# A top-2 mixture of experts: from all experts on all tokens to expert-sorted tiles with accumulating DMAs

## The chip, the cores and the metric

The kernel runs on one core of a Trainium2 chip. The metric is the device time of an execution in microseconds, the median of several runs.

## The reference

Eight sublayers in a row work on x of 4 x 256 tokens by 256 features, each as x = x + f(layernorm(x)): linear attention, mixture of experts, a convolution with a scan, the same mixture of experts again, softmax attention, attention with a routed feed-forward, delta-rule attention, and attention with a routed feed-forward again. The change is to the mixture of experts (8 experts, top 2 of them, hidden size 512), which is run twice with the same weights:

```python
x = hidden_states.reshape(-1, H)                      # 1024 tokens, H = 256
logits = SOFTCAP * jnp.tanh(x @ w_gate / SOFTCAP)     # 8 experts
probs = jax.nn.softmax(logits, axis=-1)
_, idx = jax.lax.top_k(probs, TOPK)                   # TOPK = 2
weights = probs * jax.nn.one_hot(idx, E).sum(-2)
for e in range(E):
    h = jax.nn.silu(x @ w1[e]) * (x @ w3[e])
    out = out + h @ w2[e] * weights[:, e:e + 1]
```

## The kernel before

x lives in SBUF for the whole kernel as X (128 partitions, 8 blocks of tokens, 256). `norm` writes the normalized tokens to XN and, transposed with TensorE, to XT. Each sublayer is a Stage with its own buffers and semaphores; it ends with `all_engine_barrier` (L87), so no work of one stage starts before the last of the one before it. DMAs in flight are held up by it only if an engine waits for them.

`moe` starts with the router: 16 small matmuls (L425), tanh and exp on ScalarE, then a chain of small VectorE operations (`Chain.then`: each waits for the one before it), with `top2` among them, that leaves `weight` (the probability, or zero) for every token and expert.

Then all 8 experts run over all 1024 tokens. SyncE loads an expert's w1, w3 and w2 (1.5 MB) into one of two halves of W, two experts ahead of need. Every FP32 operand is split in two fp32r parts: ScalarE casts (L476, L483, L488) and GpSimd subtracts to get the rest (L513, L518, L524). Each product is three passes (PASSES). For an expert there are 8 groups (2 halves of the tokens, 4 blocks of the hidden size) of 12 matmuls at L444, 512 columns each, then SiLU on ScalarE (L495) and the product on VectorE (L558); then 8 blocks of tokens with 12 matmuls of 256 columns at L457, each block added to X with its weight by VectorE (L562). Experts 0 and 1 are written out, the other six run in a loop.

`linear_attention` is the stage before the first mixture: L250 and L257 are its matmuls with plain FP32 operands, the first with 12 jobs of 2 matmuls. `setup` loads X and makes `ident`; its SyncE waits for X. `conv_scan` follows the first mixture. `routed_ffn` has a router of its own that calls `top2`; L956 are transposes of the softmax attention, L1635 is a small GpSimd operation in the delta attention, L562 has a register in its address.

## Time and profile before

| | |
|---|---|
| Median of 3 runs | 3173.69 us (3169.89 to 3178.28) |
| The profiled execution, its own time | 3158.17 us |
| Its span, first to last instruction | 3156.5 us |
| Mean granted clock of TensorE | 0.842 |
| TensorE matmul busy | 2496.7 us (79%) |
| TensorE weight load busy | 2058.7 us (65%) |
| VectorE, ScalarE, GpSimd busy | 1757.7, 1215.6, 1385.2 us |
| DMA | 198.73 MB, mean 63 GB/s |

PE is TensorE's matmuls and PEld its weight loads, DVE VectorE, ACT ScalarE, POOL GpSimd, SP SyncE; a q behind a name is that engine's queue or sequencer. Times are microseconds from the span's start unless they are marked otherwise. A granted clock of 1.00 is 2.4 GHz, 0.50 is 1.2 GHz. A busy share over the whole span averages stages that run one after the other and are limited by different things, so each stage has to be read by itself.

### The profile page before, as it was taken

How to read it: one execution, taken by the hardware profiler on the slowest of the kernel's cores; microseconds unless marked ns; L12 is line 12 of the kernel's file. 1: busy time of each engine (PE TensorE's matmuls, PEld its weight loads, DVE VectorE, ACT ScalarE, POOL GpSimd, SP SyncE). 2: the span in 40 equal slices, each digit the busy share in tenths (PEclk: the TensorE clock that was granted, in tenths of full speed). 3: DMA queues.
4: the chain of work that ended last, by engine and by line, in shares of the span. 5: the costliest groups of instructions: out<-in, count | busy, mean ns of one | idle time of the engine just before them, and what ended most of it. 6: DMA issues, size and time to landing. Idle time of an engine off the chain costs nothing. (4 is left out here: it accounts for less than half of the span.)

```text
span 3156.5 us, 45390 instructions
## 1 busy us (share of the span) xinstructions
PE 2496.7 (79%) x16778; PEld 2058.7 (65%) x16778; DVE 1757.7 (56%) x3323; ACT 1215.6 (39%) x2736; POOL 1385.2 (44%) x1063
## 2 busy tenths in 40 slices
PE   6699846999797988957478966796679857759798
PEld 4689725888474667846466855686567746627687
DVE  2422375222455553366867776776687687445533
ACT  2333232333241333336344643464345534213233
POOL 0454313454201005536964496637692696310064
PEclk9799967999898998979587967697668957779899
DMA  0210002110000005033321232223223332010050
GB/s 30 81 61 20 0 17 80 41 40 0 17 1 19 1 5 194 0 74 110 121 88 68 78 124 95 86 92 97 97 81 105 95 128 81 31 45 1 36 164 14
DMA packets 121569, 198.73 MB, mean 63 GB/s; under 512 B 60049, under 2 KB 94753, under 8 KB 116257
## 3 DMA queue, kind: packets, MB, share of 16 engines
q1 hardware_dynamic: 121376, 196.21, 19.2%
q8 instruction: 115, 1.88, 0.2%
q14 instruction: 78, 0.63, 0.1%
HBM read 192.38 MB, written 3.81 MB: 62 GB/s over the span
## 5 line engine op out<-in xcount | busy, mean ns | idle before, releaser
L444 PE MATMUL PS<-XP_moe,WP_moe 128*128 128x512 f32 x1536 | 355.3, 392 | 30.8 <-POOL WP_moe L518 28.6
L444 PEld LDWEIGHTS PS<-XP_moe,WP_moe 128*128 128x128 f32 x1536 | 289.6, 189 | 91.6 <-issue 28.7
L1792 PE MATMUL PS<-ident,XT 128*128 128x128 f32 x512 | 115.1, 408 | 244.8 <-DVE XT L2164 230.4
L2106 DVE SCALAR_TENSOR_TENSOR XT<-M_delta,CW_delta,XT 128x256 f32<-128x256 f32 x576 | 249.9, 495 | 71.3 <-ACT M_delta L1975 41.2
L1792 PEld LDWEIGHTS PS<-ident,XT 128*128 128x128 f32 x512 | 92.3, 211 | 264.3 <-DVE XT L2164 126.3
L1741 PE MATMUL PS<-XP_delta,X 128*128 128x268 f32 (+1 forms) x1024 | 242.0, 390 | 6.6 <-DMA X<-in_L_attn_b_heads 6.5
L558 DVE TENSOR_TENSOR HF_moe<-SG_moe,PS 128x512 f32<-128x512 f32 x128 | 87.9, 688 | 265.3 <-ACT SG_moe L495 265.2
L1741 PEld LDWEIGHTS PS<-XP_delta,X 128*128 128x128 f32 x1024 | 193.6, 190 | 56.5 <-issue 11.3
L524 POOL TENSOR_TENSOR HP_moe<-HF_moe,HP_moe 128x512 fp32r<-128x512 f32 x128 | 163.6, 1292 | 138.2 <-ACT HP_moe L488 138.2
L1019 ACT ACTIVATE PR_attn<-PS,NM_attn 128x256 f32<-128x256 f32 (+1 forms) x384 | 135.2, 419 | 224.0 <-DVE NM_attn L1079 224.0
L1256 PE MATMUL PS<-XP_rffn,UW_rffn 128*128 128x512 f32 x816 | 194.9, 396 | 4.7 <-POOL UW_rffn L1212 4.6
L1212 POOL TENSOR_TENSOR UW_rffn<-W_rffn,UW_rffn 128x512 fp32r<-128x512 f32 x34 | 43.8, 1287 | 327.0 <-ACT UW_rffn L1315 327.0
L457 PEld LDWEIGHTS PS<-WP_moe,HP_moe 128*128 128x128 f32 x1536 | 186.4, 192 | 1.2
L1680 POOL TENSOR_TENSOR DD_delta<-DD_delta,A_delta 128x64 f32<-128x64 f32 (+6 forms) x224 | 170.0, 759 | 39.2 <-ACT A_delta L2063 19.5
L457 PE MATMUL PS<-WP_moe,HP_moe 128*128 128x256 f32 x1536 | 186.8, 283 | 0.0
L1256 PEld LDWEIGHTS PS<-XP_rffn,UW_rffn 128*128 128x128 f32 x816 | 155.9, 192 | 38.5 <-issue 5.9
L945 PE MATMUL PS<-KM_attn,QK_attn 128*128 128x512 f32 x288 | 163.5, 650 | 18.7 <-DVE KM_attn L1055 18.7
L1064 DVE COPY PT_attn<-PS 128x512 f32<-128x512 f32 x144 | 99.6, 692 | 130.6 <-PE PS L956 130.6
L495 ACT ACTIVATE SG_moe<-PS 128x512 f32<-128x512 f32 x128 | 76.6, 599 | 233.8 <-PE PS L444 233.1
L1706 POOL TENSOR_TENSOR M_delta<-M_delta,DD_delta 128x2304 f32<-128x2304 f32 x32 | 164.9, 5154 | 0.0
L518 POOL TENSOR_TENSOR WP_moe<-W_moe,WP_moe 128x3072 fp32r<-128x3072 f32 x16 | 108.8, 6808 | 127.6 <-ACT WP_moe L483 127.6
L1805 PEld LDWEIGHTS PS<-XN,KQ_delta 16*128 16x128 f32 (+2 forms) x3072 | 154.5, 306 | 7.3 <-issue 7.3
(314 smaller groups left out, 5636.5 us busy)
## 6 DMA issues: line engine op xcount, KB each, us to landing
M_delta<-gram_delta SPq DMA_DIRECT2D x32, 2304.0 KB, 8.8
X<-in_L_attn_b_heads SPq DMA_DIRECT2D x64, 512.0 KB, 3.3
W_moe<-in_L_ffn_w SPq DMA_DIRECT2D x48, 512.0 KB, 4.8
CB_rffn<-routes_rffn SPq DMA_DIRECT2D x20, 512.0 KB, 23.6
XN<-in_L_attn_b_outs SPq DMA_DIRECT2D x16, 512.0 KB, 3.7
F_delta<-in_L_attn_b_outs SPq DMA_DIRECT2D x4, 2048.0 KB, 8.2
W_rffn<-in_L_ffn_tiles SPq DMA_DIRECT2D x4, 1536.0 KB, 11.6
W_rffn<-in_L_ffn_tiles SPq DMA_DIRECT2D x2, 2304.0 KB, 27.0
```

Of the source, the lines that this page charges most:

```text
L444: last = nc.tensor.matmul(PS[:, 2 * (g % 2) + i, :], up_w(qw, r, i, k, m), XP[qx][:, k, n * NB:(n + 1) * NB], start=(k + step == 0), stop= ...
L457: last = nc.tensor.matmul(PS[:, 4 + i % 4, 0:D], HP[qx][:, k, i * P:(i + 1) * P], down_w(qw, r, k), start=(k + step == 0), stop=(k == MI - ...
L524: nc.gpsimd.tensor_tensor(HP[1][:, m, n * NB:(n + 1) * NB], HF[:, g % 4, :], HP[0][:, m, n * NB:(n + 1) * NB], ALU.subtract).then_inc(hl_d, 1)
L945: nc.tensor.matmul(bank, QK[:, 0, kt, b * T + qt * P:b * T + (qt + 1) * P], KM[:, kt, h:h + per, b * T:b * T + keys], start=True, stop=False)
L1019: last = nc.scalar.activation(PR[:, u % 4, j * w:(j + 1) * w], PS[:, u % 3, j * w:(j + 1) * w], ACT.Exp, bias=NM[:, u % 4, j:j + 1])
L1256: last = nc.tensor.matmul(PS[:, 4 + 2 * n + q, :], UW[qw][:, r, (q * KD + k) * P:(q * KD + k + 1) * P], XP[qx][:, k, n * NB:(n + 1) * NB], ...
L1680: last = nc.gpsimd.tensor_tensor(DD[:, :, tri(t - 1) + 1:tri(t)], DD[:, :, tri(t):tri(t + 1)], step(t).broadcast_to([P, BH, C - t]), ALU.mult)
L1706: nc.gpsimd.tensor_tensor(q, q, by_h(DD[:]), ALU.mult).then_inc(mq_d, 1)
L1741: last = nc.tensor.matmul(PS[:, 1 + i, 0:B * (WIN - halo)], WH[:, r, i, k, :], XP[:, k, :, n * BT + halo:n * BT + WIN], start=(k == 0), st ...
L1792: last = nc.tensor.transpose(PS[:, 6 + r % 2, i * P:(i + 1) * P], W[:, B * h:B * (h + 1), :], core.ident[:])
L1805: last = nc.tensor.matmul(PS[:, 1 + b, h * 2 * C:(h + 1) * 2 * C].rearrange("p (q t) -> p q t", q=2), WT(o)[rows, h, :], GR[rows, o, h].re ...
L2106: nc.vector.scalar_tensor_tensor(TMP[:, r, i], RAW[:, r, i, :, tau:tau + BT], CW[:, i, h, tau:tau + 1], TMP[:, r, i], ALU.mult, ALU.add).t ...
```

## The change

The mixture computes only the chosen pairs of token and expert. The 2048 pairs are sorted by expert into slots in DRAM, each expert's share padded up to a multiple of 128, which needs at most 23 tiles of 128 slots (SLOTS = 2944).

- The weights of all 8 experts (12.6 MB) are loaded into SBUF once (`EW`), by 24 DMAs that SyncE issues in `linear_attention` behind that stage's own, and both mixtures use them. EW stays allocated until the second mixture is done.
- `setup` fills the slots in DRAM with a padding row (zeros, a row number past the tokens, 1032 bytes), writes a padding block behind `sums`, and now also waits for this second write, which is queued behind the fill.
- `moe`: SyncE also writes X to `sums` in DRAM. The router and `top2` are as before. TensorE counts the chosen pairs with nine bf16 products, VectorE works out each pair's slot and each tile's expert (`owner`). GpSimd issues 16 indirect DMAs, one for each block of tokens and rank, that scatter the normalized tokens with row number and weight (XW) to the slots. When all have landed SyncE loads the 23 tiles back in 5 groups (XS).
- TensorE reads the 23 owners into registers, and for each tile transposes the tokens (2), makes gate and up products (2 matmuls of 512 columns each, plain FP32), transposes the hidden rows (4), and makes the down product (4 matmuls of 256 columns). The weights' address depends on the register. ScalarE does SiLU and scales the answer, VectorE the product and the copies out of PSUM.
- GpSimd adds each tile's answers to the tokens' rows of `sums` with one indirect accumulating DMA, and waits for each to land before it issues the next. When all 23 have landed SyncE loads X back from `sums`. In the first mixture SyncE fills the slots again, behind the loads of the tiles.
- In `conv_scan` CUM no longer has a buffer of its own but lies in XP. `top2` returns the one-hot pair, and the two operations that followed it are in its callers.

The diff, with the removed lines of `moe` (all in the printed function above) and the allocations left out:

```diff
...
+EXPERT = 512
+SLOTS = 2 * N + (E - 1) * P
...
+    def expert_weights(self, ctx):
+        nc = self.nc
+        self.EW = ctx.enter_context(nc.sbuf_tensor("EW", [P, E, 3 * KD * EXPERT], FP32))
+        self.pad = ctx.enter_context(nc.sbuf_tensor("pad", [P, D + 2], FP32))
+        self.row_id = ctx.enter_context(nc.sbuf_tensor("row_id", [P, NT + 1], FP32))
+        self.slots = nc.dram_tensor("slots", (SLOTS, D + 2), FP32, kind="Internal").ap()
+        self.sums = nc.dram_tensor("sums", (N + P, D), FP32, kind="Internal").ap()
...
+    def fill_slots(self, sp):
+        sp.dma_start(self.slots.rearrange("(t p) d -> p t d", p=P),
+                     self.pad[:].unsqueeze(1).broadcast_to([P, SLOTS // P, D + 2])).then_inc(self.zeroed, 16)
+    def load_experts(self, sp):
+        if self.asked:
+            return
+        self.asked = True
+        I = EXPERT
+        for e in range(E):
+            for i, (w, k, n) in enumerate((("w1", KD, I), ("w3", KD, I), ("w2", I // P, D))):
+                sp.dma_start(self.EW[:, e, i * KD * I:(i + 1) * KD * I].rearrange("p (k n) -> p k n", k=k),
+                             self.a["L0_ffn_" + w][e].rearrange("(k p) n -> p k n", p=P)).then_inc(self.expert_in, 16)
...
         def _(sp):
             sp.dma_start(core.X[:], core.a["L0_attn_a_x"].rearrange("b (i p) d -> p (b i) d", p=P)).then_inc(x_in, 16)
-            sp.wait_ge(x_in, 16)
...
+            core.fill_slots(sp)
+            sp.dma_start(core.sums[N:N + P], core.pad[:, 0:D]).then_inc(x_in, 16)
+            sp.wait_ge(x_in, 32)
...
         def _(pool):
+            nc.gpsimd.memset(core.pad[:], 0.0).then_inc(filled, 1)
+            nc.gpsimd.iota(core.row_id[:], [[P, NT + 1]], base=0, channel_multiplier=1,
+                           allow_small_or_imprecise_dtypes=True).then_inc(filled, 1)
...
+            nc.gpsimd.tensor_copy(core.pad[:, D:D + 1], core.row_id[:, NT:NT + 1]).then_inc(filled, 1)
...
         def _(sp):
...
                 sp.dma_start(W[:, i], a["L0_attn_a_" + name].rearrange("(k p) n -> p k n", p=P)).then_inc(w_in, 16)
+            core.load_experts(sp)
...
-def top2(core, s, dve, c, p, weights, rank):
+def top2(core, s, dve, c, p, rank):
...
             src = rest
-    c.then(nc.vector.tensor_tensor(oh[:, 0], oh[:, 0], oh[:, 1], ALU.add))
-    return nc.vector.tensor_tensor(weights, oh[:, 0], p[:], ALU.mult)
+    return oh
 def moe(core, a="L0_ffn_"):
...
+    I = EXPERT
...
+    TILES = SLOTS // P
...
+    GROUPS = (0, 1, 3, 7, 13, TILES)
...
         def _(sp):
...
+            sp.dma_start(sums, X[:]).then_inc(base_out, 16)
+            core.load_experts(sp)
+            sp.wait_ge(g_in, 16)
+            sp.wait_ge(placed, 32 * NT * (layer_no + 1))
+            for i in range(len(GROUPS) - 1):
+                at = slice(GROUPS[i], GROUPS[i + 1])
+                sp.dma_start(XS[:, at], slots[:, at]).then_inc(x_in[i], 16)
+            for i in range(len(GROUPS) - 1):
+                sp.wait_ge(x_in[i], 16)
+            if layer_no == 0:
+                core.fill_slots(sp)
+            sp.wait_ge(added, 16 * TILES * (layer_no + 1))
+            sp.dma_start(X[:], sums).then_inc(x_back, 16)
+            sp.wait_ge(x_back, 16)
+        @block.gpsimd
+        def _(pool):
+            c = Chain(pool, chain_p)
+            nc.gpsimd.memset(ones[:], 1.0)
+            nc.gpsimd.memset(lower[:], float(P))
+            c.then(nc.gpsimd.memset(before[:], 1.0))
+            nc.gpsimd.affine_select(out=before[:], in_=before[:], compare_op=ALU.is_ge, fill=0.0, base=-1,
+                                    pattern=[[1, P]], channel_multiplier=-1).then_inc(consts, 1)
+            nc.gpsimd.affine_select(out=lower[:], in_=lower[:], compare_op=ALU.is_ge, fill=0.0, base=-1,
+                                    pattern=[[1, E], [-1, E]], channel_multiplier=0).then_inc(consts, 1)
+            pool.wait_ge(slot_d, 1)
+            pool.wait_ge(core.zeroed, 16 * (layer_no + 1))
+            pool.wait_ge(rows_d, 2)
+            for i in range(NT):
...
+                    nc.gpsimd.indirect_dma_start(
+                        core.slots[:], bass.IndirectOffsetOnAxis(ap=slot[:, r, i:i + 1], axis=0),
+                        XW[:, r, i], None).then_inc(placed, 16)
+            pool.wait_ge(base_out, 16)
+            for t in range(TILES):
+                if t in GROUPS:
+                    pool.wait_ge(token_d, GROUPS.index(t) + 1)
+                pool.wait_ge(y_ev, t + 1)
+                if t or layer_no:
+                    pool.wait_ge(added, 16 * (TILES * layer_no + t))
+                nc.gpsimd.indirect_dma_start(core.sums[:], bass.IndirectOffsetOnAxis(ap=token[:, t:t + 1], axis=0),
+                                             XS[:, t, 0:D], None, compute_op=ALU.add).then_inc(added, 16)
...
         def _(pe):
...
+            pe.wait_ge(consts, 2)
+            pe.wait_ge(pick_d, 1)
+            m = picked[:].rearrange("p i e -> p (i e)")
+            nc.tensor.matmul(PS[:, 6, 0:NT * E], ones[:], m, start=True, stop=True).then_inc(sum_mm, 1)
+            nc.tensor.matmul(PS[:, 5, 0:NT * E], before[:], m, start=True, stop=False)
+            for i in range(1, NT):
+                last = nc.tensor.matmul(PS[:, 5, i * E:NT * E], ones[:], m[:, 0:(NT - i) * E], start=False, stop=i == NT - 1)
+            last.then_inc(sum_mm, 1)
+            pe.wait_ge(owner_d, 1)
+            e = [pe.value_load(owner[0:1, t:t + 1], min_val=0, max_val=E - 1) for t in range(TILES)]
+            pe.wait_ge(core.expert_in, 48 * E)
+            def turn(t):
+                if t in GROUPS:
+                    pe.wait_ge(x_in[GROUPS.index(t)], 16)
+                if t:
+                    pe.wait_ge(xk_d, t)
+                for k in range(KD):
+                    last = nc.tensor.transpose(PS[:, 0, k * P:(k + 1) * P], XS[:, t, k * P:(k + 1) * P], core.ident[:])
+                last.then_inc(xt_mm, 1)
+            def gate(t):
+                pe.wait_ge(xk_d, t + 1)
+                if t >= 2:
+                    pe.wait_ge(silu_d, t - 1)
+                for k in range(KD):
+                    last = nc.tensor.matmul(PS[:, 2 + 2 * (t % 2), :], XK[:, t % 3, k],
+                                            EW[:, bass.ds(e[t], 1), k * I:(k + 1) * I].rearrange("p o n -> p (o n)"),
+                                            start=(k == 0), stop=(k == KD - 1))
+                last.then_inc(gate_mm, 1)
+            def up(t):
+                if t >= 2:
+                    pe.wait_ge(h_d, t - 1)
+                for k in range(KD):
+                    last = nc.tensor.matmul(PS[:, 3 + 2 * (t % 2), :], XK[:, t % 3, k],
+                                            EW[:, bass.ds(e[t], 1), (KD + k) * I:(KD + k + 1) * I].rearrange("p o n -> p (o n)"),
+                                            start=(k == 0), stop=(k == KD - 1))
+                last.then_inc(up_mm, 1)
+            def turn_hidden(t):
+                pe.wait_ge(h_d, t + 1)
+                if t:
+                    pe.wait_ge(ht_d, t)
+                for k in range(MI):
+                    last = nc.tensor.transpose(PS[:, 1, k * P:(k + 1) * P], H[:, t % 2, k * P:(k + 1) * P], core.ident[:])
+                last.then_inc(ht_mm, 1)
+            def down(t):
+                pe.wait_ge(ht_d, t + 1)
+                if t >= 2:
+                    pe.wait_ge(y_ev, t - 1)
+                for k in range(MI):
+                    at = 2 * KD * I + k * D
+                    last = nc.tensor.matmul(PS[:, 6 + t % 2, 0:D], HT[:, t % 2, k],
+                                            EW[:, bass.ds(e[t], 1), at:at + D].rearrange("p o n -> p (o n)"),
+                                            start=(k == 0), stop=(k == MI - 1))
+                last.then_inc(dn_mm, 1)
+            turn(0)
+            turn(1)
+            for t in range(TILES):
+                gate(t)
+                if t:
+                    turn_hidden(t - 1)
+                up(t)
+                if t + 2 < TILES:
+                    turn(t + 2)
+                if t:
+                    down(t - 1)
+            turn_hidden(TILES - 1)
+            down(TILES - 1)
...
         def _(act):
+            nc.scalar.copy(XW[:, 0, :, 0:D], XN[:])
+            nc.scalar.copy(XW[:, 1, :, 0:D], XN[:]).then_inc(rows_d, 1)
...
+            def answer(t):
+                act.wait_ge(dn_mm, t + 1)
+                nc.scalar.activation(XS[:, t, 0:D], PS[:, 6 + t % 2, 0:D], ACT.Copy,
+                                     scale=XS[:, t, D + 1:D + 2]).then_inc(y_ev, 1)
+            for t in range(TILES):
+                act.wait_ge(gate_mm, t + 1)
+                if t >= 2:
+                    act.wait_ge(h_d, t - 1)
+                nc.scalar.activation(SG[:, t % 2], PS[:, 2 + 2 * (t % 2), :], ACT.Silu).then_inc(silu_d, 1)
+                if t:
+                    answer(t - 1)
+            answer(TILES - 1)
...
         def _(dve):
...
+                nc.vector.memset(rank[:, e:e + 1], float(E - e))
+                last = nc.vector.memset(edges[:, e:e + 1], float(P * e))
+            for t in range(TILES):
+                last = nc.vector.memset(tile_at[:, t:t + 1], float(P * t))
...
+            oh = top2(core, s, dve, c, prob, rank)
+            nc.vector.tensor_tensor(picked[:], oh[:, 0], oh[:, 1], ALU.add).then_inc(pick_d, 1)
+            c.then(nc.vector.tensor_tensor(chosen[:], oh[:], prob[:].unsqueeze(1).broadcast_to([P, 2, NT, E]), ALU.mult))
+            c.then(nc.vector.tensor_reduce(weight[:], chosen[:], AX.X, ALU.add))
+            nc.vector.tensor_copy(XW[:, :, :, D + 1], weight[:])
+            for r in range(2):
+                last = nc.vector.tensor_copy(XW[:, r, :, D], core.row_id[:, 0:NT])
+            last.then_inc(rows_d, 1)
+            dve.wait_ge(sum_mm, 1)
+            dve.wait_ge(consts, 2)
+            c.then(nc.vector.tensor_reduce(count[:], PS[:, 6, 0:NT * E].rearrange("p (i e) -> p e i", e=E), AX.X, ALU.add))
+            c.then(nc.vector.tensor_tensor(over[:], count[:].unsqueeze(2).broadcast_to([P, E, E]),
+                                           edges[:].unsqueeze(1).broadcast_to([P, E, E]), ALU.is_gt))
+            c.then(nc.vector.tensor_reduce(used[:], over[:], AX.X, ALU.add))
+            c.then(nc.vector.tensor_tensor(over[:], lower[:], used[:].unsqueeze(1).broadcast_to([P, E, E]), ALU.mult))
+            c.then(nc.vector.tensor_reduce(base[:], over[:], AX.X, ALU.add))
+            dve.wait_ge(sum_mm, 2)
+            c.then(nc.vector.tensor_tensor(place[:], PS[:, 5, 0:NT * E].rearrange("p (i e) -> p i e", e=E),
+                                           base[:].unsqueeze(1).broadcast_to([P, NT, E]), ALU.add))
+            c.then(nc.vector.tensor_tensor(chosen[:], oh[:], place[:].unsqueeze(1).broadcast_to([P, 2, NT, E]), ALU.mult))
+            c.then(nc.vector.tensor_reduce(where[:], chosen[:], AX.X, ALU.add))
+            nc.vector.tensor_copy(slot[:], where[:]).then_inc(slot_d, 1)
+            c.then(nc.vector.tensor_tensor(past[:], tile_at[:].unsqueeze(2).broadcast_to([P, TILES, E - 1]),
+                                           base[:, 1:E].unsqueeze(1).broadcast_to([P, TILES, E - 1]), ALU.is_ge))
+            c.then(nc.vector.tensor_reduce(sought[:], past[:], AX.X, ALU.add))
+            nc.vector.tensor_copy(owner[:], sought[:]).then_inc(owner_d, 1)
+            def tokens(i):
+                dve.wait_ge(x_in[i], 16)
+                nc.vector.tensor_copy(token[:, GROUPS[i]:GROUPS[i + 1]], XS[:, GROUPS[i]:GROUPS[i + 1], D]).then_inc(token_d, 1)
+            def columns(t):
+                dve.wait_ge(xt_mm, t + 1)
+                if t >= 3:
+                    dve.wait_ge(up_mm, t - 2)
+                nc.vector.tensor_copy(XK[:, t % 3].rearrange("p k n -> p (k n)"), PS[:, 0, 0:D]).then_inc(xk_d, 1)
+            def hidden_columns(t):
+                dve.wait_ge(ht_mm, t + 1)
+                if t >= 2:
+                    dve.wait_ge(dn_mm, t - 1)
+                nc.vector.tensor_copy(HT[:, t % 2].rearrange("p k n -> p (k n)"), PS[:, 1, :]).then_inc(ht_d, 1)
+            columns(0)
+            columns(1)
+            tokens(0)
+            tokens(1)
+            for t in range(TILES):
+                if t:
+                    hidden_columns(t - 1)
+                dve.wait_ge(up_mm, t + 1)
+                dve.wait_ge(silu_d, t + 1)
+                if t >= 2:
+                    dve.wait_ge(ht_mm, t - 1)
+                nc.vector.tensor_tensor(H[:, t % 2], SG[:, t % 2], PS[:, 3 + 2 * (t % 2), :], ALU.mult).then_inc(h_d, 1)
+                if t + 2 < TILES:
+                    columns(t + 2)
+                if t + 2 in GROUPS[2:-1]:
+                    tokens(GROUPS.index(t + 2))
+            hidden_columns(TILES - 1)
...
-    CUM = s.sb("CUM", [P, KD, N])
+    CUM = XP[:].rearrange("p k b t -> p (k b t)")[:, 0:KD * N]
...
-            c.then(nc.vector.tensor_tensor_scan(flat(CUM), KEEP[:], flat(VR), 0.0, ALU.mult, ALU.add))
+            c.then(nc.vector.tensor_tensor_scan(CUM, KEEP[:], flat(VR), 0.0, ALU.mult, ALU.add))
...
-            c.then(nc.vector.tensor_tensor(flat(VR), flat(CUM), flat(A2), ALU.mult))
+            c.then(nc.vector.tensor_tensor(flat(VR), CUM, flat(A2), ALU.mult))
...
-            top2(core, s, dve, c, prob, weight[:, :, 0:E], rank).then_inc(route_d, 1)
+            oh = top2(core, s, dve, c, prob, rank)
+            c.then(nc.vector.tensor_tensor(oh[:, 0], oh[:, 0], oh[:, 1], ALU.add))
+            nc.vector.tensor_tensor(weight[:, :, 0:E], oh[:, 0], prob[:], ALU.mult).then_inc(route_d, 1)
...
 def program(nc, args, out):
...
         core = Core(nc, ctx, args)
...
+        core.expert_weights(experts)
...
         subs = [sub1, sub2, sub3, sub2, sub5, sub6, sub7, sub6]
-        for f in subs[START:STOP]:
+        for i, f in enumerate(subs[START:STOP]):
             f()
+            if START + i == min(3, STOP - 1):
+                experts.close()
...
```

## Rows read from the trace of the kernel before

**Rows 1.** Busy time by stretch (windows), all engines; the header names the columns.

```profile
core 0: us, PE busy (x) PEld busy (x) DVE busy (x) ACT busy (x) POOL busy (x), PEclk, DMA share, GB/s
...
121.90:383.80 261.90, 261.23 (x1512) 231.86 (x1512) 74.23 (x127) 87.26 (x132) 122.51 (x70) 1.00 0.09 30
89.90:99.00 9.10, 6.88 (x32) 6.88 (x32) 0.00 (x0) 0.95 (x1) 0.00 (x0) 0.50 0.87 274
...
820.00:1060.00 240.00, 205.63 (x1045) 0.91 0.02 7
```

**Rows 2.** Timeline where the first mixture stage ends and the second begins and ends.

```profile
384.48 1.28 ACT L196 ACT_TABLE_LOAD   x1 [10.82 <-PEq L87]
...
501.06 0.37 SPq L403 DMA_DIRECT2D WG_moe<-in_L_ffn_w_gate  x1
...
794.79 1.28 ACT L196 ACT_TABLE_LOAD   x1 [10.83 <-PEq L87]
```

**Rows 3.** Timeline of the first mixture stage's start: start, us, engine, line, op, tiles.

```profile
89.56 0.37 SPq L403 DMA_DIRECT2D WG_moe<-in_L_ffn_w_gate  x1
...
99.49 0.22 DVE L544 TENSOR_REDUCE mx_moe<-logit_moe 128x8 f32<-128x64 f32 x1 [9.59 <-ACT logit_moe L471]
...
100.16 1.88 ACT L476 CAST XP_moe<-XT 128x2048 fp32r<-128x2048 f32 x1
...
102.32 4.42 DVE L358 SCALAR_TENSOR_TENSOR top_rest_moe<-top_oh_moe,prob_moe 128x64 f32<-128x64 f32 x1
...
113.42 7.54 PE L444 MATMUL PS<-XP_moe,WP_moe 128*128 128x512 f32 x24 [14.30 <-POOL WP_moe L518]
118.28 0.60 ACT L495 ACTIVATE SG_moe<-PS 128x512 f32<-128x512 f32 x1 [9.63 <-PE PS L444]
...
125.61 0.69 DVE L558 TENSOR_TENSOR HF_moe<-SG_moe,PS 128x512 f32<-128x512 f32 x1 [3.14 <-ACT SG_moe L495]
```

**Rows 4.** PE's timeline through the experts; one pair of eight.

```profile
149.89 21.95 PE L444 MATMUL PS<-XP_moe,WP_moe 128*128 128x512 f32 x96
171.68 11.68 PE L457 MATMUL PS<-WP_moe,HP_moe 128*128 128x256 f32 x96
183.19 21.95 PE L444 MATMUL PS<-XP_moe,WP_moe 128*128 128x512 f32 x96
```

**Rows 5.** Timeline row and windows of single lines (L250, L257), linear attention.

```profile
28.57 22.57 PE L250 MATMUL PS<-XT,W_linattn 128*128 128x512 f32 x48 [7.76 <-DMA W_linattn<-in_L_attn_a_Wp]
...
36.00:51.00 15.00, 15.00 (x36) 6.43 (x34) 1.00 0.00 0
...
51.00:58.20 7.20, 7.05 (x32) 5.87 (x31) 1.00 0.01 3
```

**Rows 6.** Timeline in the softmax attention, transposes at L956.

```profile
856.75 0.47 PEld L956 LDWEIGHTS PS<-ident,PR_attn 128*128 128x128 f32 x4 [0.33 <-issue]
...
857.19 0.97 PEld L969 LDWEIGHTS PS<-V_attn,PT_attn 128*128 128x128 f32 x8
...
857.50 0.69 DVE L1064 COPY PT_attn<-PS 128x512 f32<-128x512 f32 x1 [1.01 <-PE PS L956]
```

**Rows 7.** Instructions of single lines (L1635, L562): min/median/max ns.

```profile
L1635 POOL TENSOR_TENSOR RT_delta<-RT_delta,LN_delta x32: 1006/1026/1041, 1697.9 to 2752.8; 128x4 f32<-128x4 f32 x32
...
L562 DVEq FUSED_REGOPS  x96: 46/46/46, 206.6 to 793.5; - x96
```

**Rows 8.** DMA issues: count, KB each, median us from issue to landing.

```profile
y_delta<-M_delta SPq DMA_DIRECT2D x4, 256.0 KB, 3.0
X<-spill_delta SPq DMA_DIRECT2D x1, 1024.0 KB, 5.5
...
CB_rffn<-routes_rffn SPq DMA_DIRECT2D x4, 128.0 KB, 11.9
...
WG_moe<-in_L_ffn_w_gate SPq DMA_DIRECT2D x2, 8.0 KB, 2.1
```

**Rows 9.** Timeline, first work behind the setup stage.

```profile
7.01 1.28 ACT L196 ACT_TABLE_LOAD   x1 [7.01 <-PEq L87]
```

More of the change, by code:

```diff
@@ L375, in moe @@
     prob = s.sb("prob", [P, NT, E])
-    weight = s.sb("weight", [P, E, NT])
     rank = s.sb("rank", [P, E])
@@ new lines, in moe @@
+    before = s.sb("before", [P, P], BF16)
+    ones = s.sb("ones", [P, P], BF16)
+    edges = s.sb("edges", [P, E])
+    lower = s.sb("lower", [P, E, E])
+    tile_at = s.sb("tile_at", [P, TILES])
+    count = s.sb("count", [P, E])
+    over = s.sb("over", [P, E, E])
+    used = s.sb("used", [P, E])
+    base = s.sb("base", [P, E])
+    place = s.sb("place", [P, NT, E])
+    chosen = s.sb("chosen", [P, 2, NT, E])
+    slot = s.sb("slot", [P, 2, NT], mybir.dt.uint32)
+    where = s.sb("where", [P, 2, NT])
@@ new lines, in moe @@
+    base_out, x_back, rows_d, token_d = (s.sem(n) for n in ("base_out", "x_back", "rows_d", "token_d"))
+    placed, added, layer_no = core.placed, core.added, core.layer_no
+    core.layer_no += 1
+    x_in = [s.sem(f"x_in{i}") for i in range(len(GROUPS) - 1)]
+    xt_mm, xk_d, gate_mm, up_mm, silu_d, h_d, ht_mm, ht_d, dn_mm, y_ev = (s.sem(n) for n in (
+        "xt_mm", "xk_d", "gate_mm", "up_mm", "silu_d", "h_d", "ht_mm", "ht_d", "dn_mm", "y_ev"))
+    slots = core.slots.rearrange("(t p) d -> p t d", p=P)
@@ L490, in expert @@
-            def expert(j, r, first):
-                for g in range(G):
-                    act.wait_ge(up_mm, (2 * j + r) * G + g + 1)
-                    if not (first and g < 4):
-                        act.wait_ge(h_d, (2 * j + r) * G + g - 3)
-                    nc.scalar.activation(SG[:, g % 4, :], PS[:, 2 * (g % 2), :], ACT.Silu).then_inc(silu_d, 1)
-                    if g:
-                        hidden(j, r, g - 1)
-                hidden(j, r, G - 1)
-            split(0, 0, True)
@@ L2288, in program @@
         core = Core(nc, ctx, args)
+        experts = ExitStack()
+        core.expert_weights(experts)
         setup(core)
```

153 lines of the change are left out of this document (27 added, 126 removed).

## Prediction, made before the change was built or run

> **What bounds the kernel now.** The windows by stage come first [rows 1]. The eight sublayers run one after the other with a barrier behind each, so a stage's gain is whole and nothing outside it moves. The two mixture stages are the stretches from 89.56 us (the router weights' load) to 384.48 us (first work of the next norm) and from 501.06 to 794.79 us [rows 2, 3]: 294.9 and 293.7 us, mean 294.3, together 588.6 of the 3156.5 us span. Within them read PE: from 121.9 us on it is busy 261.2 of 261.9 us at a granted clock of 1.00 [rows 1], each expert costing 21.95 us for 96 matmuls at L444 and 11.68 us for 96 at L457, a period of 33.3 us [rows 4]. Eight experts are 266 us; the other 28 us are routing, splitting the first weights, and a slow start. So PE sets the end, and what counts is how many columns PE streams, plus whatever stands before its first tile and behind its last.
>
> **What is removed.** All 8 x 33.3 us of dense matmuls, with the splits and casts on ACT, DVE and POOL. Those lay beside PE except before the first expert: there PE waits 14.3 us for POOL's split. DVE's routing chain also has an operation stretched to 4.42 us beside POOL's large subtractions, against 0.22 us for another of its size [rows 3]. With no large POOL work in the new stage I expect none of that.
>
> **The tile loop.** The new matmuls take plain FP32 operands in one pass instead of three split ones. The plain FP32 stage shows the price: L250 needs 12 x 2 matmuls of 512 columns and the trace has 48 records, so two records each; a stretch of 15.0 us with PE never idle holds 34 loads and touches 36 matmul records, so some 35 pitches of 0.429 us. L257's 32 records of 256 columns span 7.05 us, 0.220 each [rows 5]. Four transposes in a row start their loads at 856.75 and give way at 857.19: 0.11 us each [rows 6]. A tile has 4 matmuls of 512 columns (8 records, 3.43 us), 4 of 256 (8 records, 1.76) and 6 transposes (0.66): 5.85 us, times 23 is 134.5. I add 3 us per layer for the start (24 matmuls took 7.54 us at first, against 0.227 each later [rows 3, 4]) and 0.15 us a tile for gaps, 3.4: 140.9 us. The order gate(t), turn_hidden(t-1), up(t), turn(t+2), down(t-1) leaves each result of another engine one matmul group of at least 1.7 us: the product on DVE costs 0.69 us, SiLU on ACT 0.60 [rows 3], the copy of the turned hidden rows 0.69 [rows 6]. DVE has at most three such copies and products a tile, 2.1 us, ACT at most 1.2, so neither is late. Register arithmetic for the dynamic weight offset has 46 ns an operation on DVE's sequencer [rows 7]; three or four beside a matmul of 0.44 or 0.86 us stay hidden, and cost some 0.2 us each if they aren't.
>
> **Before the first tile.** From stage start to the first DVE reduction is 9.9 us as before [rows 3]. Its ten small chained operations up to 102.32 with ACT's exponential among them take 2.83 us, so some 0.255 each and 0.3 more; 31 of them come to 8.3 us, and the slots stand 18.2 us after the start. The constants, ACT's two copies of XN (near 1.9 us each by the cast of that size) and PE's nine counting products lie under the router's matmuls and the DVE chain. Then POOL issues 16 indirect scatters one after the other, which no row shows. Below, SP's issue of a DMA is 0.37 us; above, a full landing of 3.0 us each [rows 3, 8]. I take 1.2, just over the 1.03 us that a POOL operation on 4 elements costs [rows 7], its fixed cost: 19.2 us (ends 6 and 48). The last scatter lands 3.0 us later, SP issues the gathers in 0.4, the first two groups land 3.0 later: 6.4. Two transposes and a copy: 1.2. PE's 23 register loads wait only on the owners and lie under the scatters. Sum 45.0 us.
>
> **Behind the last tile.** Product, copy, answer and their hand-overs 1.7; the last accumulating DMA L; SP's issue 0.35, the 1 MB reload of X 5.5 [rows 8], barrier 0.3. For L the bounds are 2.1 us (the landing of an 8 KB load) and 11.9 (a 128 KB broadcast load), the nearest row is the 3.0 us of a 256 KB store; since an addition must read before it writes I take nearly twice that, 5.5 us. Together 13.4.
>
> The Trainium skill ("DMA: Bandwidth & Descriptors", section on the anatomy of a DMA on the SWDGE path) gives such a DMA about 2.0 us plus its bytes over 436 GB/s, an estimate of 2.3 us here; no row of this trace has such a DMA. By it the layer would end 3.2 us sooner and the kernel 6.4 us sooner.
>
> **Outside the stages.** Setup now waits for a 128-row store queued behind a 3.04 MB fill of the slots. At the 274 GB/s of the busiest stretch [rows 1] the fill is 11 us, behind most of X's own load, with which setup ended at 7.0 before [rows 9]; it should now end near 17.5: +10.5 us (ends +5 and +20). The 12.6 MB of expert weights need 46 us at that rate, from 28.6 us on, where the stage's own weights have landed [rows 5], plus the 10.5: done near 85, before the mixture stage's loads, then near 100, want the rings. The second fill and 24 loads less in each layer lie under PE. CUM's new place and the split-up top2 cost nothing: same operations in the same chain.
>
> **Sum.** A layer: 45.0 + 140.9 + 13.4 = 199.3 us against 294.3, so 95.0 less; twice is 190.0; less 10.5 leaves 179.5. The profiled execution took 3158.17 us (span 3156.5), so 2978.7. The median of the three timed runs is 3173.69, 15.5 above it, and carried over that gives **2994 us**.
>
> **Rivals.**
> Rival A, the chain of accumulating DMAs sets the end. Each waits for the one before it, so 23 L run in series. The first answer comes at 45.0 + 3 + two tiles (12.0) + 0.5 = 60.5 us, the last at 187.6, so above L = 5.8 us the chain is the bound, and the layer takes 66.7 + 23 L. My 5.5 is barely under. For it: a row's read, addition and write in series, with 128 KB loads at 11.9 us in this trace; against it: plain stores at 3.0 [rows 8]. At 8 us: 250.7 a layer, 3097 us in all. Chance 0.27 up to the next case.
> Rival B, the same chain on the other side: slower from L = 9.7 us, where 66.7 + 23 L reaches 289. At the 11.9 us bound: 340.4 a layer, 3276 us. Chance 0.05.
> Rival C, dispatch costs more: 3.0 us for each scatter adds 28.8 a layer, 3052 us. Chance 0.05.
> Rival D, PE keeps its lower clock (1.2 GHz) through the loop. A fifth of the tile's instructions are transposes and the groups are short. Against: the attention stretch, mixed in the same way with transposes and waits, was granted 0.91 [rows 1, 6]. The price is PE's 134.5 us again, less the 3 already counted: +131.5 a layer, 3257 us. Chance 0.03.
> The Trainium skill ("TensorE: Matmul & The Clock Gate", Part 4 on transposes) says that transposes don't count as busy PE for the clock in the same way. By that rule D's time would follow if they weighed enough; the trace doesn't bear it out for attention, which stayed at 0.91.
>
> **How the numbers follow.** My own case has 0.60; its range is 2950 (scatters at 0.4 us, no gaps, L of 3, setup +5) to 3035 (scatters at 2.0, setup +20). The whole range goes from 2945 into rival A up to just over L = 8: 3100, leaving out some 0.05 below and 0.13 above. About 0.3% is what a measurement of this kernel can tell. Faster: own case, A and C, 0.92. Slower: B, D and small change, 0.07. Within 0.3%: 0.01.
>
> **What would show it.** In the profile after: L444 and L457 gone; 184 matmuls (368 records) and 138 transposes a layer in some 138 us at clock near 1.00; PE idle from the counting products for about 29 us while POOL's queue shows 16 issues; accumulating DMAs spaced at PE's pace (6 us), not at their own landing time. If they are evenly spaced above 6 us, and PE's last tile ends well before the last of them, A was right and the step "L" was mis-sized. If the tile period is near 9 or 12 us with a granted clock of 1.00 or 0.50, the loop's price was. Setup's end tells the fill.

## The result, and the profile after

The changed kernel takes 2977.45 us (median of 4 runs, 2967.05 to 2982.18), the kernel before, run beside it, 3171.79 (4 runs, 3167.83 to 3178.28). The ratio is 0.938, with an interval of 0.935 to 0.941. The forecast was 2994 us in a range of 2945 to 3100: it was 17 us, 0.6%, too high, on the right side and by the right mechanism. The profiled execution took 2972.99 us.

The page of the changed kernel: the head, the costliest group that is new, and the DMA issues. The columns are those of the page before.

```profile
span 2971.3 us, 40960 instructions
...
PE 2231.3 (75%) x14736; PEld 1748.9 (59%) x14736; DVE 1663.0 (56%) x3309; ACT 1082.8 (36%) x2558; POOL 1211.4 (41%) x1008
...
L506 POOL DMA_INDIRECT sums<-XS_moe,token_moe x46 | 71.7, 1560 | 220.6 <-ACT XS_moe L602 201.6
...
EW<-in_L_ffn_w SPq DMA_DIRECT2D x24, 512.0 KB, 10.5
...
slots<-pad SPq DMA_DIRECT2D x2, 2967.0 KB, 14.3
...
X<-sums SPq DMA_DIRECT2D x2, 1024.0 KB, 5.4
...
sums<-XS_moe,token_moe POOLq DMA_INDIRECT x46, 3.8
```

L506 is the accumulating DMA, 46 of them, 23 for each layer. Of the 220.6 us that POOL idled ahead of them, 201.6 ended with ACT's answer (L602). So the adds wait mostly for the tiles and not for one another. This one line already speaks against rival A.

The second view is the timeline of the changed kernel: setup, then the first mixture stage from its first row (102.63) to its first and last tiles, and the starts of the next norm.

```profile
1.58 0.36 SPq L80 DMA_DIRECT2D slots<-pad  x1
...
1.99 8.66 SPq L134 DMA_DIRECT2D sums<-pad  x1
...
19.03 1.28 ACT L237 ACT_TABLE_LOAD   x1 [19.03 <-PEq L120]
...
102.63 0.37 SPq L465 DMA_DIRECT2D WG_moe<-in_L_ffn_w_gate  x1
...
113.20 0.22 DVE L624 TENSOR_REDUCE mx_moe<-logit_moe 128x8 f32<-128x64 f32 x1 [9.36 <-ACT logit_moe L595]
...
121.26 1.24 POOL L496 DMA_INDIRECT slots<-XW_moe,slot_moe  x1 [17.58 <-DVE slot_moe L653]
122.79 0.97 POOL L496 DMA_INDIRECT slots<-XW_moe,slot_moe  x1 [0.30 <-issue]
...
140.54 0.96 POOL L496 DMA_INDIRECT slots<-XW_moe,slot_moe  x1 [0.30 <-issue]
143.28 2.46 SPq L472 DMA_DIRECT2D XS_moe<-slots  x5
...
145.48 0.66 PE L535 MATMUL PS<-ident,XS_moe 128*128 128x128 f32 x2 [27.05 <-DMA XS_moe<-slots]
...
158.52 1.88 PE L543 MATMUL PS<-EW,XK_moe 128*128 x4
...
160.24 0.60 PE L562 MATMUL PS<-ident,H_moe 128*128 128x128 f32 x4
...
160.68 1.88 PE L552 MATMUL PS<-EW,XK_moe 128*128 x4
...
162.39 0.38 PE L535 MATMUL PS<-ident,XS_moe 128*128 128x128 f32 x2
...
162.61 1.89 PE L571 MATMUL PS<-EW,HT_moe 128*128 x8
...
283.80 0.47 ACT L602 ACTIVATE XS_moe<-PS,XS_moe 128x256 f32<-128x256 f32 x1 [2.82 <-PE PS L571]
285.84 1.55 POOL L506 DMA_INDIRECT sums<-XS_moe,token_moe  x1 [3.03 <-DMA sums<-XS_moe,token_moe]
289.71 0.36 SPq L478 DMA_DIRECT2D X<-sums  x1
295.95 1.28 ACT L237 ACT_TABLE_LOAD   x1 [11.68 <-PEq L120]
...
412.75 0.37 SPq L465 DMA_DIRECT2D WG_moe<-in_L_ffn_w_gate  x1
...
605.62 1.28 ACT L237 ACT_TABLE_LOAD   x1 [11.43 <-PEq L120]
```

Read three things here. The stage lasts from 102.63 to 295.95, 193.3 us, and the second from 412.75 to 605.62, 192.9; before they were 294.9 and 293.7 [rows 2]. The 16 scatters stand in one row behind the other, each 0.96 us (the first 1.24) and 0.30 of issue, and PE waits 27.05 us through them. And none of the five PE rows of a tile (158.52 to 162.61) has a bracket: nothing was waited for. The next gate follows at 164.34, 5.82 us behind the last one.

The third view is busy time by stretch, for the changed kernel: the expert loads beside the linear attention, and the tile loop.

```profile
core 0: us, PE busy (x) PEld busy (x) DVE busy (x) ACT busy (x) POOL busy (x), PEclk, DMA share, GB/s
60.00:70.00 10.00, 10.00 (x38) 6.96 (x37) 0.00 (x0) 5.27 (x10) 0.00 (x0) 1.00 1.07 372
150.00:280.00 130.00, 130.00 (x487) 79.87 (x486) 38.31 (x69) 23.70 (x44) 32.75 (x21) 1.00 0.30 55
```

PE is still what sets the loop, busy in all of 130 us at a granted clock of 1.00, as it was before [rows 1]. It only has fewer columns to stream.

The clock is not at 1.00 from the first matmul on. Over the scatters PE is busy 8.89 of 45 us, and the loop starts at the lower level:

```profile
100.00:145.00 45.00, 8.89 (x48) 8.34 (x46) 8.88 (x74) 7.92 (x8) 16.65 (x21) 0.50 0.22 75
147.30:151.00 3.70, 3.70 (x7) 1.59 (x6) 0.56 (x3) 0.04 (x1) 0.00 (x0) 0.53 1.07 362
```

```profile
147.33 3.60 PE L543 MATMUL PS<-EW,XK_moe 128*128 x4
```

The first tile's gate products take 3.60 us where those of later tiles take 1.88. The price is 1.7 us a layer.

Where the time went, from spans: the two stages 588.65 to 386.2, 202.5 less. Against that: setup ends at 19.03 where it was 7.01 [rows 9], +12.0; the linear attention with the norm behind it is 1.1 us longer (68.6 against 67.5); the stretch between the two mixtures is 0.2 longer. The part behind the second mixture, which the change doesn't touch, took 2365.7 us against 2361.7, +4.0. 202.5 - 12.0 - 1.1 - 0.2 - 4.0 is 185.2, and the spans differ by as much (3156.5 - 2971.3). That last stretch, the same code in every kernel of this study, took between 2355.1 and 2375.0 us. Differences of a few us are therefore read from the stages below and not from totals.

### The profile page after: what moved, and what is told of

It reads as the page before. It is cut to its first block and busy times, and to the rows that moved or that the text cites. A ratio compares the mean times of both kernels' runs of the same rounds, so it can differ in the third digit from the quotient of the medians.

```text
span 2971.3 us, 40960 instructions
## 1 busy us (share of the span) xinstructions
PE 2231.3 (75%) x14736; PEld 1748.9 (59%) x14736; DVE 1663.0 (56%) x3309; ACT 1082.8 (36%) x2558; POOL 1211.4 (41%) x1008
## 3 DMA queue, kind: packets, MB, share of 16 engines
q8 instruction: 113, 1.85, 0.3%
## 5 line engine op out<-in xcount | busy, mean ns | idle before, releaser
L1864 PEld LDWEIGHTS PS<-XP_delta,X 128*128 128x128 f32 x1024 | 193.1, 190 | 55.8 <-issue 10.7
L506 POOL DMA_INDIRECT sums<-XS_moe,token_moe x46 | 71.7, 1560 | 220.6 <-ACT XS_moe L602 201.6
L1928 PE MATMUL PS<-XN,KQ_delta 16*128 16x16 f32 (+2 forms) x3072 | 154.0, 349 | 0.0
L2200 ACT ACTIVATE S_delta<-S_delta,AO_delta 128x128 f32<-128x128 f32 x512 | 152.1, 390 | 0.0
L1496 DVE TENSOR_TENSOR SU_rffn<-PS,CB_rffn 128x512 f32<-128x512 f32 x68 | 47.0, 691 | 178.9 <-PE PS L1377 158.3
L1895 PE MATMUL PS<-KQ_delta,TR_delta 128*128 128x64 f32 x1024 | 136.3, 280 | 13.7 <-DVE TR_delta L2246 13.6
L1895 PEld LDWEIGHTS PS<-KQ_delta,TR_delta 128*128 128x128 f32 x1024 | 131.4, 201 | 18.1 <-DVE TR_delta L2246 18.1
L1090 PEld LDWEIGHTS PS<-V_attn,PT_attn 128*128 128x128 f32 x1152 | 140.3, 192 | 0.2
L1342 POOL TENSOR_TENSOR HP_rffn<-HF_rffn,HP_rffn 128x512 fp32r<-128x512 f32 x68 | 92.4, 1378 | 115.8 <-ACT HP_rffn L1459 115.8
## 6 DMA issues: line engine op xcount, KB each, us to landing
EW<-in_L_ffn_w SPq DMA_DIRECT2D x24, 512.0 KB, 10.5
W_rffn<-in_L_ffn_tiles SPq DMA_DIRECT2D x4, 1536.0 KB, 12.6
```

What stands on the lines that cost most here:

```text
L1090: last = nc.tensor.matmul(o, PT[:, u % 4, (j * (qt + 1) + t) * P:(j * (qt + 1) + t + 1) * P], V[:, 2 * b + t, kt * HK + h + j, :], start=( ...
L1864: last = nc.tensor.matmul(PS[:, 1 + i, 0:B * (WIN - halo)], WH[:, r, i, k, :], XP[:, k, :, n * BT + halo:n * BT + WIN], start=(k == 0), st ...
L1895: last = nc.tensor.matmul(PS[:, 5 * (g % 2), i * 2 * OC:(i + 1) * 2 * OC].rearrange("p (q t) -> p q t", q=2), TR[:, g % 3, i * P:(i + 1) * ...
L1928: last = nc.tensor.matmul(PS[:, 1 + b, h * 2 * C:(h + 1) * 2 * C].rearrange("p (q t) -> p q t", q=2), WT(o)[rows, h, :], GR[rows, o, h].re ...
L2200: last = nc.scalar.activation(S[:, lane, :], S[:, lane, :], ACT.Copy, scale=AO[:, lane:lane + 1])
```

## Experiments

The open questions after this profile: is it PE's columns that set the stage, and how far is the chain of adds from taking over; what does the staggered order buy; are the scatters worth their issue time and no more; and can the loss at setup be had back.

**A second chained add per tile (double_add).** Behind each add comes one more, of zeros to the same rows, so that the chain has 46 links.

```
                     XS[:, t, 0:D], None, compute_op=ALU.add).then_inc(added, 16)
+                pool.wait_ge(added, 16 * (2 * TILES * layer_no + 2 * t + 1))
+                nc.gpsimd.indirect_dma_start(core.sums[:], bass.IndirectOffsetOnAxis(ap=token[:, t:t + 1], axis=0),
+                                             core.pad[:, 0:D], None, compute_op=ALU.add).then_inc(added, 16)
```

> Behind each tile's accumulating DMA stands a second one to the same rows, chained to the first, that adds zeros. Theory (the chain of adds is a resource beside PE with about 4.5 us a round, hidden under PE's 5.82 us a tile): the chain now needs 9.0 us a tile and becomes the bound; a layer goes from 193.1 us to 57.4 + 22 x 9.0 + 8.4 + 6.3 = 270 us, the whole to about 3127 us, with adds evenly spaced at 4.5 and PE's loop unchanged at 5.82 a tile. Rival (adds are hidden whatever they cost, since PE sets the end): only the last tile's second add shows, 4.5 us a layer, 2982 us.

It took 3113.15 us, span 3111.4, near the 3127 of the chain's theory (a link came out shorter than the 4.5 us assumed) and far from the other's 2982. The stages are 265.1 us (101.61 to 366.75) and 258.8 (483.85 to 742.62), 71.8 and 65.9 more. POOL's timeline in the first of them, and two windows:

```profile
172.15 1.56 POOL L506 DMA_INDIRECT sums<-XS_moe,token_moe  x1 [2.99 <-DMA sums<-pad,token_moe]
176.27 1.55 POOL L509 DMA_INDIRECT sums<-pad,token_moe  x1 [2.55 <-DMA sums<-XS_moe,token_moe]
180.78 1.55 POOL L506 DMA_INDIRECT sums<-XS_moe,token_moe  x1 [2.97 <-DMA sums<-pad,token_moe]
```

```profile
150.00:280.00 130.00, 130.00 (x491) 80.23 (x489) 38.31 (x69) 23.82 (x45) 42.55 (x28) 1.00 0.35 61
280.00:360.00 80.00, 2.25 (x11) 1.46 (x9) 0.69 (x1) 0.81 (x2) 29.06 (x19) 0.54 0.28 31
```

Here is what rival A would have looked like. These adds are released by the DMA before them, 4.1 to 4.5 us apart, and so are all of the layer's 46 but the first and one more, while PE runs through the loop as before and is then busy for 2.25 of 80 us. One link is 4.37 us on average ((360.5 - 159.3) / 46), and 4.29 without the first, which took 8.25. Two chained links of the changed kernel itself are 4.50 and 4.55 (168.84, 173.34 and 177.89 us). With one add for each tile the chain needs less than the tile's 5.82 us, so it hides, by a margin of 1.3 to 1.5 us a tile.

**One rounded pass on PE (one_pass).** The weights, the turned tokens and the turned hidden rows are typed fp32r, so that a matmul is one record in place of two. The products are rounded by this.

```
-        self.EW = ctx.enter_context(nc.sbuf_tensor("EW", [P, E, 3 * KD * EXPERT], FP32))
+        self.EW = ctx.enter_context(nc.sbuf_tensor("EW", [P, E, 3 * KD * EXPERT], PART))
...
-    XK = s.sb("XK", [P, 3, KD, P])
+    XK = s.sb("XK", [P, 3, KD, P], PART)
...
-    HT = s.sb("HT", [P, 2, MI, P])
+    HT = s.sb("HT", [P, 2, MI, P], PART)
```

> The tile loop's matmuls take float32r operands in one rounded pass (EW, XK and HT declared float32r), so they leave out the precision of plain FP32; all else as in the changed kernel. PE's matmuls shrink from 5.2 to about 1.4 us a tile, with the transposes about 2.1 us. Theory (two parallel limits: PE at 5.82 us a tile, the chain of adds at 4.4 to 4.5): the chain sets the end, adds evenly spaced near 4.45; a layer is 50 + 22 x 4.45 + 3.9 + 6.3 = 158 us, the whole about 2904 us. Rival 1 (PE alone matters): 23 x 3.7 us a layer less, about 2803 us. Rival 2 (VectorE and ScalarE turn into the bound above 4.5 us a tile): adds spaced wider than their landing, over 2910 us.

It took 2904.43 us, span 2902.6. PE's timeline and then POOL's for the same tiles, and the group of the adds:

```profile
175.28 0.75 PE L571 MATMUL PS<-EW,HT_moe 128*128 x4 [0.17 <-DVE HT_moe L673]
...
177.92 0.75 PE L571 MATMUL PS<-EW,HT_moe 128*128 x4 [0.18 <-DVE HT_moe L673]
```

```profile
173.16 1.55 POOL L506 DMA_INDIRECT sums<-XS_moe,token_moe  x1 [2.99 <-DMA sums<-XS_moe,token_moe]
177.88 1.55 POOL L506 DMA_INDIRECT sums<-XS_moe,token_moe  x1 [3.17 <-DMA sums<-XS_moe,token_moe]
```

```profile
L506 POOL DMA_INDIRECT sums<-XS_moe,token_moe x46 | 71.7, 1559 | 162.6 <-DMA sums<-XS_moe,token_moe 114.9 <-ACT XS_moe L602 47.6
```

A tile now goes through PE in 2.64 us, the adds come 4.7 us apart (4.4 to 4.9 over both layers, but for the first two links of the first), and 114.9 us of POOL's idle time end with a DMA where 201.6 us ended with ACT. From outside, PE lost more than half of its tile and the stage only gave back 24.8 us in the first layer (168.5) and 32.3 in the second (160.6): the bound has gone over to the chain. The first layer is 8 us longer than the second. Its first adds lie beside the second fill of the slots, a 3 MB store: they stand at 153.33, 162.63 and 168.61 us, 9.3 and 6.0 apart, where the second layer, which has no fill, has 4.5 and 4.8. That is 6 of the 8 us; the other 2 are ahead of the first add. The same fill delays the changed kernel's second add to 8.9 us behind the first (159.98 to 168.84); by the fifth add (182.75) the chain has caught up with the tiles and nothing is lost. It depends on where the fill falls: in tiles_17 below it is issued 3 us sooner (151.76 us against 154.71), and no link is stretched.

That the total hits the expected 2904 is luck. The stages were forecast at 158 us each and took 168.5 and 160.6, 13 us more in all; the stretch behind the second mixture was 10.5 us shorter than in the changed kernel (2355.1), and what stands ahead of the first mixture was 1.2 shorter.

**The tile's work in line (in_line).** PE does turn_hidden(t) and down(t) right behind up(t), without the stagger over the next tile; ACT and DVE follow the same order.

```
                 gate(t)
-                if t:
-                    turn_hidden(t - 1)
                 up(t)
...
-                if t:
-                    down(t - 1)
-            turn_hidden(TILES - 1)
-            down(TILES - 1)
+                turn_hidden(t)
+                down(t)
```

> TensorE's order is changed to gate(t), up(t), turn(t+2), turn_hidden(t), down(t), so nothing of another tile stands between a product and its use. Theory (the old order hides VectorE's product and copy, each 0.69 us with about 0.2 us of hand-over on either side): 0.9 us of waiting before turn_hidden and 1.1 before down, 7.8 us a tile instead of 5.82, 46 tiles, +92 us, about 3065 us, at a granted clock of 1.00. Rival 1: the waits pull the granted clock down as well, and a tile takes over 9 us. Rival 2: the order is worth nothing and the time stays within 9 us.

It took 3052.72 us, span 3051.0, 12 us less than expected; the stages are 237.1 and 235.6 us, 43.8 and 42.7 more. One tile on PE's timeline, and the loop's window:

```profile
179.92 1.88 PE L552 MATMUL PS<-EW,XK_moe 128*128 x4
181.64 0.38 PE L535 MATMUL PS<-ident,XS_moe 128*128 128x128 f32 x2
182.58 0.66 PE L562 MATMUL PS<-ident,H_moe 128*128 128x128 f32 x4 [0.56 <-DVE H_moe L678]
184.11 1.99 PE L571 MATMUL PS<-EW,HT_moe 128*128 x8 [0.87 <-DVE HT_moe L667]
185.93 1.88 PE L543 MATMUL PS<-EW,XK_moe 128*128 x4
187.65 1.02 PE L552 MATMUL PS<-EW,XK_moe 128*128 x2
```

```profile
150.00:280.00 130.00, 105.65 (x373) 61.53 (x372) 29.32 (x54) 17.63 (x33) 25.32 (x17) 1.00 0.24 45
```

The period is 7.73 us (179.92 to 187.65), 1.91 more. The two brackets, the product and then the copy on DVE, make 1.43 of it. The other 0.48 is in the spacing of groups beside a stall, which no longer overlap their neighbours: the hidden transposes take 0.66 where the next group came 0.44 us behind them in the staggered loop, the token transposes 0.38 against 0.22, the down products 1.82 against 1.73. So the stagger is worth 43 us a layer, and the clock stayed at 1.00 with PE idle a fifth of the loop: what was lost was time waited, not frequency.

**Half of the scatters (half_scatter).** Leaves out the scatters of each token's second choice, so that those rows of the slots stay padding.

```
             for i in range(NT):
-                for r in range(2):
+                for r in range(1):
```

> Leaves out the 8 scatters of the second choices in each layer; their slots hold the padding row, and all 23 tiles are computed as before. Theory (the 16 scatters are issued in series at 1.27 us and all lie on the path): 8 x 1.27 x 2 = 20.3 us less than the kernel after, about 2953 us. Rival (the landing of the rows or the counting ahead of them sets the wait, the issue is hidden): less than 5 us gained.

It took 2952.81 us. The gather is issued 30.8 us behind the stage's start (102.79 to 133.57) where it was 40.65, so 9.9 us sooner, or 1.23 for each scatter left out. The stages are 184.8 and 184.7 us, 8.5 and 8.2 less. Most of the issue time lies bare on the path, about 1 us for each scatter. That the total hits the expected 2953 is partly luck: the stages give 16.7 us, and the stretch behind them 4.7, of which 1.2 is lost elsewhere.

Why 8.5 us and not 9.9? PE starts its first tile later behind the gather than before, 4.39 us behind its issue against 2.20, and its wait ends with no other engine's work (2.2 us are lost by it; the first gate products, 2.80 us instead of 3.60, give 0.8 back):

```profile
137.96 0.66 PE L535 MATMUL PS<-ident,XS_moe 128*128 128x128 f32 x2 [18.86 <-issue]
```

In both layers this start lies 15.5 us behind the end of the cast that writes the owners (122.42 to 137.96, 423.55 to 439.13). What PE has to do between the two is to read the 23 owners into registers, some 0.68 us each by this estimate; no row shows the reads themselves, so this is inferred. In the changed kernel 23.7 us lie between the two, so the reads are hidden, as the prediction had it. But they stand close behind the scatters: fewer or cheaper scatters alone gain no more than about 8 us a layer.

**Seventeen tiles (tiles_17).** Leaves out the last six tiles of both layers.

```
-    TILES = SLOTS // P
+    TILES = 17
```

> Leaves out the last 6 of the 23 tiles in both layers. Theory (PE sets the loop at 5.82 us a tile, everything ahead and behind is fixed): 6 x 5.82 x 2 = 69.8 us less, about 2903 us by the profiled execution's 2973. Rival (another cost that doesn't grow with tiles hides part of the loop, such as a chain that catches up at the end): less than 60 us.

It took 2898.85 us. The stages are 159.1 and 156.5 us, 34.2 and 36.4 less, together 70.6 for 12 tiles: 5.88 us each. By layer it is 5.70 and 6.07; a stage of one and the same kernel differs by 0.7 us between two executions (193.3 and 194.0 in the first layer, 192.9 and 192.2 in the second, after and after_again). Within that, a tile costs what PE takes for it.

**The padding store ahead of the fill (pad_first).** At setup, the 128-row store that setup waits for is issued first.

```
             sp.wait_ge(filled, 3)
-            core.fill_slots(sp)
             sp.dma_start(core.sums[N:N + P], core.pad[:, 0:D]).then_inc(x_in, 16)
+            core.fill_slots(sp)
             sp.wait_ge(x_in, 32)
```

> In setup the store of the padding block to sums is issued before the fill of the slots instead of behind it; all else is the kernel after. My theory: setup waits for that store only because it sits behind 3.04 MB in the same rings, so setup ends at 7.0 to 7.6 us instead of 19.03, the fill lands under the norm before the stage's weights are asked for at 22, and the kernel takes 11.5 to 12 us less than the kernel after (profiled 2972.99, so about 2961). Rival: the fill's traffic only moves, and the norm or the linear attention gives back more than half: less than 6 us gained.

It took 2960.17 us (4 runs, 2954.79 to 2964.60), 0.934 of the kernel before, 0.931 to 0.938. The timeline of its setup, and the start of its first mixture:

```profile
1.57 0.34 SPq L133 DMA_DIRECT2D sums<-pad  x1
...
1.96 0.43 SPq L80 DMA_DIRECT2D slots<-pad  x1
8.27 1.28 ACT L237 ACT_TABLE_LOAD   x1 [8.27 <-PEq L120]
...
91.09 0.37 SPq L465 DMA_DIRECT2D WG_moe<-in_L_ffn_w_gate  x1
```

Setup ends at 8.27 us, later than the 7.0 to 7.6 expected, and the mixture starts 11.5 us sooner. The fill is still there. Whether the 1.3 us over the 7.01 of before are its doing was not tried. SP's issue of the padding store is 0.34 us now; behind the fill it took 8.66.

**The expert loads later as well (pad_and_loads).** pad_first, and the expert loads behind the linear attention's wait for its own weights, and the store of X to the sums behind the router weights' landing.

```
-            core.load_experts(sp)
             sp.wait_ge(w_in, 80)
+            core.load_experts(sp)
...
+            sp.wait_ge(g_in, 16)
             sp.dma_start(sums, X[:]).then_inc(base_out, 16)
             core.load_experts(sp)
-            sp.wait_ge(g_in, 16)
```

> The padding store ahead of the fill, as in pad_first, and two more edits: the linear attention asks for the experts' weights only when its own have landed, and the mixture stores X to sums only when the router's weights have landed. Theory (both cost by sharing the rings with a load that PE waits for: the linear attention's wait grew from 6.55 to 7.75 us, the router's from 2.56 to 3.20 us): 1.2 + 2 x 0.6 = 2.4 us less than pad_first, 14 us less than the changed kernel. Rival: these waits are not from sharing, and nothing beyond the 12 us of pad_first is gained; or the later start of 12.6 MB reaches into the first mixture and costs.

It took 2958.88 us (5 runs, 2955.61 to 2971.12), 0.935, interval 0.9326 to 0.9366. That is no gain over pad_first: the second mixture starts at 401.18 us here and at 401.19 there. Its window over the router weights' load:

```profile
91.00:94.50 3.50, 0.00 (x0) 0.00 (x0) 1.13 (x39) 3.47 (x2) 0.96 (x5) 0.50 0.08 9
```

PE waits 3.5 us for 8 KB with the DMA engines at 0.08. I had put the longer wait (from the stage's start to PE's first matmul 3.2 us in the changed kernel, 2.6 before) down to sharing with the other transfers, and that fell. Its cause is open.

**The changed kernel again (after_again).** No edit; 5 runs, to place the last two against it.

> The changed kernel once more, unchanged, beside the other kernels of this call. It should take 2977 us within 0.3%.

2975.22 us (2967.71 to 2982.14), 0.940, interval 0.9372 to 0.9421. The intervals of after_again and pad_and_loads do not meet, so the better order at setup is a gain. The medians put it at 16 us; up to the end of the second mixture the two profiled executions differ by 11.8 us (606.14 and 594.36), and the rest is the noisy stretch behind. pad_first and pad_and_loads can't be told apart; they are the fastest versions here that compute the same thing in full precision.

## Why the prediction was right, and where its numbers were off

**What bounds.** Right. PE set the stage before and sets it after. Three experiments agree on it: the tiles left out were worth 5.88 us each, an order that costs PE 1.91 us a tile lengthens the stage by 23 times that, and fewer PE records shorten it until another bound is met.

**The tile loop.** 5.85 us was forecast from two records for a 512-column FP32 matmul and 0.11 us for a transpose, and the tile took 5.82. The allowance of 0.15 us a tile for gaps was not needed: of the last answer's end at 284.27, 136.9 us lie behind the first gate matmul (147.33), where 140.9 and 1.7 for the hand-over were forecast. The 3 us allowed for a slow start were 1.7, at a granted clock of 0.53. PE shows no wait in any tile of the two layers but the last (0.87 us ahead of its down products, at 281.77 in the first), so the register arithmetic for the dynamic offset was hidden as assumed. The next line is that group for the changed kernel; min, median and max in ns:

```profile
L543 PEldq FUSED_REGOPS  x92: 46/46/51, 146.8 to 582.8; - x92
```

**Before the first tile.** Sum 45.0 forecast, 44.7 measured (102.63 to 147.33), from parts that cancel a little: the slots at 18.6 against 18.2; the scatters 20.2 against 19.2 (1.27 us each against 1.2); last landing and gather 4.0 against 6.4; turn and copy 1.85 against 1.2. DVE's chain ran at 0.25 us an operation, without the 4.42 us one of before [rows 3], as expected with POOL idle.

**Behind the last tile.** L, the landing of an accumulating DMA, was mis-sized: 5.5 us forecast, 3.8 measured, with 4.4 us from one issue to the next when they are chained. It came out of two bounds, 2.1 and 11.9 us, and was a guess between them. The total behind the last answer is 11.7 us, as forecast (13.4 less the 1.7 counted above), because the last add waited 1.57 us for the one before it (284.27 to 285.84) and the reload with its issue and the barrier took 6.24 against 6.15. The estimate of 2.3 us by the Trainium skill's formula ("DMA: Bandwidth & Descriptors", anatomy of a DMA) was lower than the trace by 1.5 us, mine was higher by 1.7.

**Outside the stages.** Setup +12.0 against +10.5. Of this 10.8 comes from the padding store's place behind the fill, which pad_first gave back. The expert loads reached 372 GB/s where 274 were assumed, and were done by 80 us, under the linear attention. That stage with the norm behind it grew by 1.1 us, which the sum had at nothing; 0.3 of it is left in pad_first and less than 0.1 in pad_and_loads, one profiled execution each.

**The sum.** A layer 193.1 against 199.3, twice 12.4 us too high; setup 1.5, the linear attention 1.1, the stretch between 0.2 and the noisy stretch 4.0 too low: 5.6 us too high by these parts against 5.7 by the profiled execution (2978.7 forecast, 2972.99). The other 11 of the 17 us come from carrying over the 15.5 us by which the median of before lay above its profiled execution; for the changed kernel that distance is 4.5. What varies there was not tried.

**The rivals.** Rival A was not the case, but its mechanism is real and its threshold fits: a link of 4.4 us stays under the threshold of 5.8, and in double_add and one_pass, where the balance is tipped from either side, the chain does set the end. No run tries a steady link near 5.8 us, so the threshold itself is worked out and not measured. Rival B needs 9.7 us for every link; the longest that was seen is 9.5 us (in_line), and only the second add of a first layer came near that, beside the fill. Rival C: 1.27 us a scatter, not 3.0. Rival D: the granted clock was 1.00 from the second tile on with six transposes in a tile, and 1.00 too with PE idle a fifth of the time (in_line); the lower level was there only for the first 3.7 us of the loop, and cost 1.7. The transposes are 6 of a tile's 22 records, more than the fifth that the prediction gives, but only 0.66 of its 5.82 us. So this is no test of what the Trainium skill ("TensorE: Matmul & The Clock Gate", Part 4) says of transposes, which did not come to bear here. The upper end of the prediction's own case, 3035, is 3029 by the terms that it names.

## What to carry to other kernels

When a stage is bound by PE's columns, count the columns: two records per FP32 matmul of 512 columns, from any row with the same operand type, gave the new loop to 0.5%. When a change puts a chain of dependent DMAs beside the loop, work out the link length at which the chain takes over, since this is the number that matters; here 4.4 us a link hides under a 5.8 us tile, but every later improvement of the tile below some 4.5 us is lost, and a large store beside the chain can double a link. And look at what a short transfer that somebody waits for is queued behind: one reordered line was worth 11.5 us.
